# A two-layer convolution kernel: batch norms finished inside the next stage, and the third convolution ending with pair 0

## The reference, cut to what matters

```python
def _L0(x, ...):                       # x: (64, 1024, 14, 14) f32
    out = relu(_bn(_conv(x, w1), g1, be1))            # 1x1, 1024 -> 256
    out = relu(_bn(_conv(out, w2), g2, be2))          # 3x3, 256 -> 256
    out = _bn(_conv(out, w3), g3, be3)                # 1x1, 256 -> 1024
    return relu(x + softplus(residual_scale)[0] * out)
    # _bn takes mean and variance of a channel over all 64 images
def _L1(x, ...):
    out = relu(group_norm(conv(x, w1)))               # 1x1, 1024 -> 256
    om = conv(out, w_off, pad=1) + b_off              # 27 channels: offsets and mask
    sampled = bilinear_sample(out, py, px) * mask     # 9 taps, deformable
    out = relu(group_norm(einsum(sampled, w2)))       # 256 -> 256
    return relu(group_norm(conv(out, w3)) + x)        # 1x1, 256 -> 1024
```

## Time and profile before

| | us |
|---|---|
| median of 3 runs | 3158.97 |
| lowest and highest | 3150.49, 3162.46 |
| the profiled execution | 3153.34 |
| its span, first to last instruction | 3151.6 |
| PE busy in the span | 2998.2 |
| DVE busy | 2310.0 |
| ACT busy | 1807.0 |
| POOL busy | 738.7 |
| mean granted clock of PE | 0.980 |

### The profile page before, as it was taken

One profiled execution on the slowest core, in us unless ns is written; L12 is line 12 of the kernel. 1 busy time (PEld: TensorE's weight loads), 2 busy tenths in 40 slices (PEclk: granted clock), 3 DMA queues, 4 the chain that ended last, 5 costly groups with the idle time before them and its releaser, 6 DMA issues.

```text
span 3151.6 us, 47048 instructions
## 1 busy us (share of the span) xinstructions
PE 2998.2 (95%) x16864; PEld 2936.3 (93%) x16864; DVE 2310.0 (73%) x4756; ACT 1807.0 (57%) x3313; POOL 738.7 (23%) x455
## 2 busy tenths in 40 slices
PE   8998999998998499999999999999999999999996
PEld 8998999998998399999999999999999999999996
DVE  4655555544565468888888888888888888888885
ACT  4444222224665356666666766776667666766664
POOL 0000000000000133333333333333333333333331
PEclk9999999999999599999999999999999999999998
DMA  6553000002554334444444444444444444444431
GB/s 227 185 189 115 1 1 1 1 1 103 208 211 177 123 120 152 140 144 154 154 140 147 149 152 144 148 155 141 153 149 154 139 155 151 150 141 154 151 114 72
DMA packets 190681, 414.89 MB, mean 132 GB/s; under 512 B 17552, under 2 KB 160880, under 8 KB 185584
## 3 DMA queue, kind: packets, MB, share of 16 engines
q1 hardware_dynamic: 144368, 309.11, 28.6%
q10 hardware_dynamic: 46080, 102.78, 10.2%
HBM read 296.42 MB, written 115.40 MB: 131 GB/s over the span
## 4 chain that ended last, share of the span: by engine, by line
PE 51%; DVE 14%; ACT 1%; DMA 1%; issue 0%; POOL 0%; SPq 0%; ACTq 0%; POOLq 0%; DVEq 0%
PE work L69 6%; PE work L71 6%; PE work L70 6%; PE sample L69 6%; PE deform L69 5%; PE sample L70 5%; PE sample L71 5%; PE deform L70 5%; PE deform L71 5%; DVE x L1279 3%; DVE x L1166 3%; DVE s_lo L1261 2%; DVE x_lo L1172 2%; DVE v_lo L1269 2%; DVE aT_lo L1252 1%; PE work L1416 1%
## 5 line engine op out<-in xcount | busy, mean ns | idle before, releaser
L1127 POOL TENSOR_TENSOR hats<-hats 98x784 f32<-98x784 f32 (+1 forms) x320 | 625.9, 1956 | 821.9 <-DMA hats<-hat_scratch 787.0
L989 ACT ACTIVATE v_hi<-sample 128x392 fp32r<-128x392 f32 (+1 forms) x640 | 295.8, 462 | 325.4 <-PE sample L71 303.9
L69 PE MATMUL sample<-s_hi,aT_hi 98*128 98x392 f32 (+1 forms) x1280 | 428.2, 335 | 21.2 <-DVE s_lo L1261 18.1
L69 PE MATMUL deform<-v_hi,w_w 128*128 128x392 f32 x1152 | 409.6, 356 | 15.4 <-DVE v_lo L1269 15.4
L70 PE MATMUL sample<-s_lo,aT_hi 98*128 98x392 f32 (+1 forms) x1280 | 421.5, 329 | 0.0
L71 PE MATMUL sample<-s_hi,aT_lo 98*128 98x392 f32 (+1 forms) x1280 | 420.3, 328 | 0.0
L70 PE MATMUL deform<-v_lo,w_w 128*128 128x392 f32 x1152 | 392.1, 340 | 0.0
L71 PE MATMUL deform<-v_hi,w_w 128*128 128x392 f32 x1152 | 391.8, 340 | 0.0
L1269 DVE TENSOR_TENSOR v_lo<-sample,v_hi 128x392 fp32r<-128x392 f32 (+1 forms) x640 | 326.3, 517 | 69.8 <-ACT v_hi L989 68.8
L1261 DVE TENSOR_TENSOR s_lo<-hats,s_hi 98x784 fp32r<-98x784 f32 (+1 forms) x320 | 332.8, 1040 | 11.6 <-ACT s_hi L980 10.1
L980 ACT ACTIVATE s_hi<-hats 98x784 fp32r<-98x784 f32 (+1 forms) x320 | 251.8, 787 | 115.2 <-DVE x L1166 77.0
(11 more groups left out here) (147 smaller groups left out, 7473.7 us busy)
## 6 DMA issues: line engine op xcount, KB each, us to landing
hats<-hat_scratch SPq DMA_DIRECT2D x768, 150.1 KB
x_in<-in_x SPq DMA_DIRECT2D x32, 1568.0 KB, 6.4
y_scratch<-y_out SPq DMA_DIRECT2D x32, 1568.0 KB, 5.1
x<-in_x SPq DMA_DIRECT2D x64, 784.0 KB, 6.2
y_in<-y_scratch ACTq DMA_DIRECT2D x256, 196.0 KB, 2.9
out<-x ACTq DMA_DIRECT2D x64, 784.0 KB, 3.4
hats<-hat_scratch SPq DMA_DIRECT2D x192, 75.0 KB
hat_scratch<-offs_b SPq DMA_DIRECT2D x128, 96.5 KB
```

The source lines that it names most:

```text
L69: nc.tensor.matmul(out, w_hi, x_hi, start=start, stop=False)
L989: nc.scalar.activation(v_hi[:, group % 2, c, 0:taps_of(g), i, :], sample[:, t % 2, 0:cols(g)].rearrange("p (k s) -> p k s", s=PIX), ACT.Co ...
L1127: nc.gpsimd.tensor_tensor(hats[:, slot, 0:2, 0:n], hats[:, slot, 0:2, 0:n], hats[:, slot, 2:3, 0:n].broadcast_to([HALF, 2, n]), ALU.mult). ...
```

## The change

- `bn_coefficients` is gone as a block. A class `BatchNorm` keeps the statistics; `gather_early` aggregates those of the first 28 pairs while the stage is still running, and `gather`, `root` and `coefficients` run in the block of the next stage: there DVE aggregates the last 4 pairs and joins the two parts.
- In the first and third convolution the last pair is counted by DVE from PSUM, ahead of ACT's copy, in the first by half: the first half of the channels is counted when its products are done. In the second convolution the counting is split by halves of the channels.
- The first step of the second and of the third convolution is split by halves of the channels: PE begins with the first half once that is ready.
- The third convolution takes the pairs in the order 1 to 31, then 0, and does not store pair 0: its y stays in SBUF (`y_home`), and `add_y` of pair 0 reads it there. SP no longer waits for the stores at the end of the block; SP, ACT and DVE wait for them at the start of the next one. x of pair 0 is loaded by halves of the slices, not by images.
- `wo` and `w3` are still loaded at the start of the stage, but split one step later: `wo` behind `raw_a` and `coefficients` of pair 0, `w3` behind `part_om` and `rest_om` of pair 0.
- On PE all 8 `conv1` calls of pair 1 stand ahead of the first sample tile of pair 0. ACT and DVE have for that step an order of their own, `second`, in which all of pair 1's `make_x1`, `add_y` and `rest_x1` stand ahead of pair 0's first `part_s` and `rest_s`.
- The last pair's `add_x1` and `rectify` go image by image with a signal for each operation, and its output is stored in four quarters where it was two halves.
- Several buffers get another place in SBUF (`y_home`, `in_home`), and the small tensors of a norm share one.

```diff
+class BatchNorm:
+
+
+
+    EARLY = 28
+    REST = PAIRS - EARLY
...
+    def gather_early(self, dve, t):
+        dve.wait_ge(self.counted, self.EARLY)
+        ins = self.nc.vector.bn_aggr(self.early_mv[:, t, :],
+                                     self.stats[:, t, 0:self.EARLY, :].rearrange("p a b -> p (a b)"))
+        if t == self.tiles - 1:
+            self.then(dve, ins)
+            self.then(dve, self.nc.vector.tensor_scalar(self.early_var[:], self.early_mv[:, :, 1], self.EARLY / PAIRS,
+                                                        EPS, ALU.mult, ALU.add))
...
+    def gather(self, dve):
+
+        nc, v = self.nc, self.nc.vector
+        dve.wait_ge(self.counted, PAIRS)
+        for t in range(self.tiles):
+            last = v.bn_aggr(self.rest_mv[:, t, :],
+                             self.stats[:, t, self.EARLY:PAIRS, :].rearrange("p a b -> p (a b)"))
+        self.then(dve, last)
+        part = self.REST / PAIRS
+        v.scalar_tensor_tensor(self.var[:], self.rest_mv[:, :, 1], part, self.early_var[:], ALU.mult, ALU.add)
+        self.then(dve, v.tensor_tensor(self.apart[:], self.rest_mv[:, :, 0], self.early_mv[:, :, 0], ALU.subtract))
+        self.then(dve, v.scalar_tensor_tensor(self.apart2[:], self.apart[:], part * (1 - part), self.apart[:],
+                                              ALU.mult, ALU.mult))
+        v.tensor_tensor(self.var[:], self.var[:], self.apart2[:], ALU.add).then_inc(self.var_ready, 1)
+        self.then(dve, v.scalar_tensor_tensor(self.mean[:], self.apart[:], part, self.early_mv[:, :, 0],
+                                              ALU.mult, ALU.add))
+        self.then(dve, v.tensor_tensor(self.mean[:], self.mean[:], self.bias, ALU.add))
+        self.then(dve, v.tensor_tensor(self.mean[:], self.bias, self.mean[:], ALU.subtract))
+        if self.residual is not None:
+            dve.wait_ge(self.soft_step, 3)
+            self.then(dve, v.scalar_tensor_tensor(self.soft[:, 3:4], self.residual, 0.0, self.soft[:, 2:3],
+                                                  ALU.max, ALU.add))
+
+    def coefficients(self, dve):
+        v = self.nc.vector
+        dve.wait_ge(self.rstd_ready, 1)
+        self.then(dve, v.tensor_tensor(self.scale[:], self.rstd[:], self.gamma, ALU.mult))
+        self.then(dve, v.tensor_tensor(self.mean[:], self.mean[:], self.scale[:], ALU.mult))
+        if self.residual is None:
+            v.tensor_tensor(self.shift[:], self.mean[:], self.beta, ALU.add).then_inc(self.ready, 1)
+        else:
+            soft = self.soft[:, 3:4]
+            self.then(dve, v.tensor_tensor(self.shift[:], self.mean[:], self.beta, ALU.add))
+            v.tensor_scalar(self.scale[:], self.scale[:], soft, None, ALU.mult)
+            v.tensor_scalar(self.shift[:], self.shift[:], soft, None, ALU.mult).then_inc(self.ready, 1)
+        dve.wait_ge(self.ready, 1)
...
+                if pair == PAIRS - 1:
+                    act.wait_ge(norm.counted, PAIRS)
...
-                at_least(dve, h_written, pair + 1)
+                if pair < PAIRS - 1:
+                    at_least(dve, h_written, pair + 1)
                 for t in range(KM):
-                    nc.vector.bn_stats(stats[:, t, bass.ds(pair, 1), :].rearrange("p a b -> p (a b)"),
-                                       h[:, t, bass.ds(pair * PAIR, PAIR)])
+                    if pair == PAIRS - 1:
+                        dve.wait_ge(*((first_of_last, 1), (half_multiplied, 2 * PAIRS))[t])
+                    last = nc.vector.bn_stats(norm.stats[:, t, pair, :], h[:, t, bass.ds(pair * PAIR, PAIR)]
+                                              if pair < PAIRS - 1 else acc[:, pair % 2, t, 0:PAIR])
+                last.then_inc(norm.counted, 1)
...
+                if pair > norm.EARLY and pair - norm.EARLY <= KM:
+                    norm.gather_early(dve, pair - norm.EARLY - 1)
...
+        def halves(m):
+
+            return [(slice(4 * k, 4 * k + 4), 1) for k in range(KM)] if m == 0 else [(slice(0, 4 * KM), 2)]
...
+            act.wait_ge(before.ready, 1)
...
+        @block.gpsimd
+        def _(pool):
+            before.root(pool)
...
+            before.gather(dve)
...
+            before.coefficients(dve)
...
+def third_in_turn(step):
+
+    for n in range(PAIRS):
+        step(n, (n + 1) % PAIRS, n // 2, n % 2)
...
+                sp.wait_ge(y_written, 4 * n + 4)
+                if pair > 0:
+                    sp.dma_start(y3[pair], y_out[slot].rearrange("p k i s -> p k (i s)")).then_inc(y_stored[slot], 16)
+            third_in_turn(store)
...
+                    if n == PAIRS - 1:
+                        act.wait_ge(*((last_counted, q + 1) if q < 3 else (norm.counted, PAIRS)))
...
+                if n >= norm.EARLY:
+                    for t in (2 * (n - norm.EARLY), 2 * (n - norm.EARLY) + 1):
+                        norm.gather_early(dve, t)
...
+                if p.n == 0:
+                    part = slice(i * KX // 2, (i + 1) * KX // 2)
+                    sp.dma_start(x1[:, p.buf, :, part, :].rearrange("p i k s -> p i (k s)"),
+                                 x[p.n][:, :, i * KX // 2 * PIX:(i + 1) * KX // 2 * PIX]).then_inc(x_loaded[p.buf][i], 16)
+                    return
...
+            for slot in range(2):
+                sp.wait_ge(y_stored[slot], 16 * (PAIRS // 2 - slot))
...
             def load_y(p, k):
+                if p.n == 0:
+                    return
...
+            def rectify_last(p):
+                for i in range(2):
+                    for k in range(KX):
+                        act.wait_ge(added_last, i * KX + k + 1)
+                        last = nc.scalar.activation(x1[:, p.buf, i, k, :], x1[:, p.buf, i, k, :], ACT.Relu,
+                                                    bias=gn3.shift[:, i, k:k + 1])
+                        if k % (KX // 2) == KX // 2 - 1:
+                            part = slice(k + 1 - KX // 2, k + 1)
+                            last.then_inc(rectified_last, 1)
+                            act.wait_ge(rectified_last, 2 * i + k // (KX // 2) + 1)
+                            act.dma_start(out[p.n][:, i, part.start * PIX:part.stop * PIX],
+                                          x1[:, p.buf, i, part, :].rearrange("p k s -> p (k s)")
+                                          ).then_inc(out_stored[p.buf][i], 16)
...
+            def second(now, after, coming):
+                load_y(after, 1)
+                make_distance(now, 0)
+                make_distance(now, 1)
+                make_hats(now)
+                make_mask(now)
+                load_y(after, 2)
+                make_x1(after, 0)
+                load_y(after, 3)
+                make_x1(after, 1)
+                part_aT(now, 0)
+                load_y(after, 4)
+                make_x1(after, 2)
+                load_y(after, 5)
+                make_x1(after, 3)
+                part_aT(now, 1)
+                load_y(after, 6)
+                make_x1(after, 4)
+                load_y(after, 7)
+                make_x1(after, 5)
+                make_x1(after, 6)
+                make_x1(after, 7)
+                part_s(now, 0)
+                part_s(now, 1)
+                part_v(now, 0)
+                part_v(now, 1)
...
                 raw_a(after)
+                if after is not None and after.n == 0:
+                    wo.make_hi(act, wo_stage, 1)
...
                 part_om(after)
+                if after is not None and after.n == 0:
+                    w3.make_hi(act, w3_stage, 1)
...
-                if after is None and coming is not None:
-                    wo.make_hi(act, wo_stage, 1)
-                    w3.make_hi(act, w3_stage, 1)
...
+            for slot in range(2):
+                act.wait_ge(y_stored[slot], 16 * (PAIRS // 2 - slot))
+            before_layer.soften(act)
+            act.wait_ge(before_layer.ready, 1)
...
+                if p.n == 0:
+                    if k % (KX // 2) == 0:
+                        dve.wait_ge(x_loaded[p.buf][k // (KX // 2)], 16)
+                else:
+                    if k == 0:
+                        for i in range(2):
+                            dve.wait_ge(x_loaded[p.buf][i], 16 * (p.lap + 1))
+                    dve.wait_ge(y_loaded[k % 2], 16 * (KX // 2 * (p.n - 1) + k // 2 + 1))
+                from_y = y_in[:, k % 2] if p.n else y_left[:, k]
...
+            def second(now, after, coming):
+                rest_aT(now, 0)
+                add_y(after, 3)
+                rest_x1(after, 1)
+                rest_aT(now, 1)
+                add_y(after, 4)
+                rest_x1(after, 2)
+                add_y(after, 5)
+                rest_x1(after, 3)
+                add_y(after, 6)
+                rest_x1(after, 4)
+                add_y(after, 7)
+                rest_x1(after, 5)
+                rest_x1(after, 6)
+                rest_x1(after, 7)
+                rest_s(now, 0)
+                rest_s(now, 1)
...
```

(8 more changed lines are left out.)

460 lines of the change are left out of this document (286 added, 174 removed).

## The result

| kernel | median, us | range (runs) | ratio, 95% interval |
|---|---|---|---|
| before | 3158.97 | 3150.49 to 3163.06 (5) | |
| after | 3114.95 | 3113.51 to 3121.63 (5) | 0.9869, 0.985 to 0.9889 |

The change takes 44 us off. PE's row answers to the earlier trace rows: the same matmuls and the same busy time, so what went is idleness.

The account below looks back on a forecast made before the run. PE bounds the kernel, leaving only its idleness at the seams to win. Terms 3.8 + 3.9 + 25.5 - 0.4 + 6.0 + 2.0 = 40.8 off 3153.3 give 3112.5; forecast median 3115, range 3103 to 3130.

Parts of the forecast that it names:

- Seams A and B: PE's gaps between first and second, and second and third convolution: 3.8 and 3.9 us saved.
- rival 1: In the norms, aggregations do not shrink with their input; price 8.4 us, giving 3123; chance 0.10.
- Seam C: From the third convolution to pair 0 in the second layer: 25.8 us saved at `raw_a`, counted as 25.5.
- rival 4: Before pair 0, something else holds its first add and 13 us of gain are lost: 3128; chance 0.04.
- The weights: Moved split in pair 0's norm: `wo` costs nothing, `w3` 0.4 us (0 to 1.9) before `make_distance`.
- D: Pair 0's first iteration: pair 1's slices go ahead, filling PE's 8.82 us idle; 6.0 us saved, between 0 and 9.
- rival 2: Iteration 0 gains nothing or loses, through slower y loads or longer POOL collisions; price 6 to 9: 3122; chance 0.12.
- rival 3: PE keeps its upper clock over the shorter seams or through iteration 0; worth 3 to 6: 3110; chance 0.09.
- E: End of the kernel, last relus and stores: 2.2 us saved, taken as 2.0, between 1 and 3.
- rival 5: Last stage settles in another rhythm, DVE falling on POOL's products more often; slower, 3175; chance 0.08.

Follow-up runs that it names:

- `iter0_undone`: The changed kernel with iteration 0 of the last stage back in the old order on PE, ACT and DVE; 3119.5 us, ratio 0.9888.

## Why the prediction was right, and where it was not

- **Seams A and B** were right: 3.8 and 3.75 us of idleness against 3.8 and 3.9. The aggregations were taken as 0.2 each and are 0.14 to 0.20; rival 1 falls.
- **Seam C** was right at each step: idle 9.74 against 10.2, slices in 11.1 us (1013.55 to 1024.65) against 11.7. No transfer held the first add, so rival 4 falls. It came out 1.4 larger than counted, half a microsecond in each of these, the rest from counting 25.8 as 25.5.
- **The weights**: 0.4 was counted, and up to 2.0 is measured, with D's one microsecond for `w3`'s low part among it. The place mattered all the same: left where it was, the split would have cost 7.9 us by the end of pair 1's `rest_a`.
- **D failed in its size**: 1.4 against the 5.6 of D less the weights, so this part of rival 2 came true. The step is "two loads in flight of 2.9 each": 2.9 is the median of the earlier trace rows, and the very row names a longest of 5.7. The load of slice 6 took 5.5. This is no chance of one execution: in the seven profiles of kernels with this order and these loads it took 4.5 to 5.7. It lies among nine loads of hats that SP issues from 1051.21 to 1058.11. In `iter0_undone`, where it is issued 16 us later, behind a group of three, it took 2.3. So its place among the hats' loads is the likely cause, though no run moved the hats alone. With y on chip the stretch gained 5.5, and with the adds moved too, 7.5. A second cost was left out: behind the wait PE is at 1.2 GHz again, until about 1069.7.
- **The clock** (rival 3) did not stay up: behind the shorter seams the granted clock was 0.50 (300 to 304, 725.7 to 727.7 and 1014 to 1018 us), as the forecast had it, and in iteration 0 too.
- **E** was right in size (1.7 for 2.0), from the order and not from the smaller stores.
- **The long stage.** "DVE has 8 us to spare an iteration, so five more collisions cost nothing" was wrong. An `s_lo` that PE needs next costs at once, whatever DVE has to spare over an iteration; with POOL's product cut into four an iteration is 31.2/30 = 1.0 us shorter. That a last stage can settle differently (rival 5) is real: the stage took 9.4 us more in the repeat of the same kernel and up to 19 more in its variants, with 10 and 15 waits for an `s_lo` where the first profile had 5. But the runs show no part of this that belongs to the change.

The forecast of 3115 was met by 0.1 us because most of the 4.2 us that were missing in D and the weights were made up elsewhere, 2.6 of them by chance. So close a hit is luck: the same kernel took 3120.3 when it was timed again.

## What to carry over

For a transfer on which a chain hangs, take the longest landing of its row, not the median, above all when the change puts it beside other loads. Slack of an engine over an iteration says nothing about an operation that the bound engine waits for next: look at the longest of its instances, not at the mean. Where VectorE with two SBUF inputs stands beside a long GpSimd product and GpSimd has time, cut that product into several instructions: here one line brought as much as half of the whole change, and a second cut 12 to 18 us more.
